# Self attention of a decoder layer: keys, values and scales prepared in the same block as the row loop, tile by tile

## What is computed

```python
def attn(q, k, v):                      # q = layernorm(x)
    step = s // 4
    scale = q[:, ::step].reshape(b, -1) # 4 rows of each batch, 2048 numbers
    qk = jnp.einsum('bsd,btd->bst', q, k)
    softmax_qk = jax.nn.softmax(qk * scale[:, None, :], axis=-1)
    return jnp.einsum('bst,btv->bsv', softmax_qk, v)
x = x + attn(layernorm(x), K, V)
```

## Time and profile before

| | |
|---|---|
| median of 3 runs | 4042.1 us (4041.01 to 4042.7) |
| the profiled execution, its own time | 4039.45 us |
| its span in the profile | 4037.6 us |
| mean granted TensorE clock | 0.976 of full speed |
| TensorE busy over the span | 3803.5 us (94%) |
| VectorE, ScalarE, GpSimd busy | 2418.4, 1424.2, 1483.0 us |
| first block (setup) | 2.1 to about 59.8 us |
| second block (32 tiles) | 59.8 us to about 850 us |
| the rest: context, cross attention, experts | about 850 to 4037.6 us |

### The profile page before, as it was taken

The page is one execution under the profiler, slowest core; times in us unless marked ns, Lnnn a source line. Parts: engine busy times, 40 slices in busy tenths (PEclk is TensorE's granted clock), DMA queues, the critical chain, the costliest instruction groups (busy, mean ns, idle before and its releaser), DMA issues. The chain is left out here.

```text
span 4037.6 us, 63533 instructions
## 1 busy us (share of the span) xinstructions
PE 3803.5 (94%) x19001; PEld 2549.3 (63%) x19161; DVE 2418.4 (60%) x6231; ACT 1424.2 (35%) x1757; POOL 1483.0 (37%) x827
## 2 busy tenths in 40 slices
PE   4999999979997899999999999999999999997997
PEld 3888888868875544454444444444444777776885
DVE  5444444434446677887878888888887434324235
ACT  2221122223222254544545554555555222113332
POOL 1000000000002566677666667766664221310033
PEclk7999999989998999999999999999999999998999
DMA  3001100035546521122222222222111433318488
GB/s 135 31 31 36 34 31 31 31 132 186 177 159 181 146 44 39 35 48 55 55 55 55 55 55 52 55 55 55 44 30 40 159 120 114 124 63 289 164 292 285
DMA packets 224152, 381.61 MB, mean 95 GB/s; under 512 B 17016, under 2 KB 101528, under 8 KB 223900
## 3 DMA queue, kind: packets, MB, share of 16 engines
q1 hardware_dynamic: 196668, 309.73, 26.3%
q0 software_dynamic: 13120, 43.00, 2.9%
q10 hardware_dynamic: 14112, 25.70, 1.7%
HBM read 229.71 MB, written 148.66 MB: 94 GB/s over the span
## 5 line engine op out<-in xcount | busy, mean ns | idle before, releaser
L960 DVE CUSTOM_DVE_ANT_0 xf_unread<-xa_mx_ps,mask_q 128x402 bf16<-128x402 f32 x1984 | 1033.6, 573 | 302.2 <-PE xa_mx_ps L953 164.5
L1547 ACT ACTIVATE probs<-xa_scores 128x1024 f32<-128x1024 f32 (+1 forms) x416 | 417.5, 1024 | 416.4 <-PE xa_scores L1421 371.2
L1547 ACT ACTIVATE xa_probs<-xa_scores 128x1024 f32<-128x1024 f32 (+1 forms) x416 | 417.2, 1024 | 405.6 <-PE xa_scores L1421 360.3
L1382 POOL TENSOR_TENSOR xa_sums<-xa_sums,xa_probs 128x1024 f32<-128x1024 f32 x220 | 519.5, 2382 | 20.0 <-POOL xa_sums L1382 15.0
L1382 POOL TENSOR_TENSOR xa_sums<-xa_sums,probs 128x1024 f32<-128x1024 f32 x220 | 519.4, 2381 | 18.1 <-POOL xa_sums L1382 14.1
L1421 PE MATMUL xa_scores<-mask_t,ident_b 128*128 128x512 bf16 (+1 forms) x1505 | 499.8, 387 | 5.2 <-issue 0.2
L953 PE MATMUL xa_mx_ps<-xa_kp,queries 96*128 96x402 f32 x1024 | 364.6, 418 | 0.8
L953 PE MATMUL xa_mx_ps<-xf_kp,xf_qp 96*128 96x402 f32 x960 | 343.7, 419 | 0.4
L1415 PE MATMUL xa_scores<-xf_qp,xf_kp 97*128 97x512 f32 (+1 forms) x832 | 284.2, 423 | 20.9 <-ACTq L1569 13.4
L953 PEld LDWEIGHTS xa_mx_ps<-xa_kp,queries 96*128 96x128 f32 x1024 | 181.8, 189 | 169.3 <-DVE xf_maxima L960 109.2
L1415 PE MATMUL xa_scores<-queries,xa_kp 97*128 97x512 f32 (+1 forms) x832 | 284.5, 423 | 1.8 <-ACT probs L1547 1.8
(11 more groups left out here) (332 smaller groups left out, 7379.3 us busy)
## 6 DMA issues: line engine op xcount, KB each, us to landing
ex_src<-sorted_in SPq DMA_DIRECT2D x78, 256.0 KB, 2.7
sorted_out<-ex_made ACTq DMA_DIRECT2D x78, 256.0 KB, 2.5
xf_kp<-kT_high SPq DMA_DIRECT2D x16, 800.5 KB
xa_kp<-kT_high SPq DMA_DIRECT2D x16, 800.5 KB
cxl_rows<-in_ctx SPq DMA_DIRECT2D x16, 768.0 KB, 5.7
values<-cxl_v SPq DMA_DIRECT2D x48, 256.0 KB
kT_high<-cxl_kT_high SPq DMA_DIRECT2D x12, 768.0 KB, 4.0
kT_low<-cxl_kT_low SPq DMA_DIRECT2D x12, 768.0 KB, 6.2
```

What stands on the lines that cost most here:

```text
L960: return dve.tensor_tensor_reduce(out=unread[slot % 2][:, :], in0=scores[:, 0:MKEYS], in1=mask_q[:, half * QB + qt, MFIRST[kb]:MFIRST[kb] ...
L1382: pool.tensor_tensor(sums[pr][:, :, :], left[pr][:, :, :], right[pr][:, :, :], ALU.add).then_inc(pool_added, 1)
L1547: act.activation(prob[ring][pr][0:keys, :, :], scores[pr][0:keys, :, :], ACT.Exp, scale=SCALE).then_inc(exped, 1)
```

## The change

One block in place of two. K and V are loaded in 32 tiles of 256 KB into a ring of seven buffers of 2 KB a partition: the four quarters of `prob`, `out`, `x_add` and a new `spare`. K's transposes go through three PSUM banks that the loop uses later (`pT_ps` 0 and 1, `o_ps`) instead of eight. The first tile's scores stand between the transposes of K. The scale rows are loaded batch by batch: those of batch 0 behind the first four tiles of K, the others (1 MB each) behind V. The statistics and the normalization of batches 1 to 3 stand inside tiles 0 to 3 of VectorE, which are written out for this. `exp(0)` waits until all of V is split, since it writes the buffers that V comes through. The low part of V is subtracted tile by tile, the even ones by VectorE, the odd ones by GpSimd.

```diff
-        self_attention_setup(nc, ident, x, k, v, kT, vs, scale)
-        self_attention_loop(nc, ident, x, x1, kT, vs, scale, NB, KB, tiles)
+        raw = [prob[:, j, :] for j in range(NB)] + [out[:, :], x_add[:, :], spare[:, :]]
+        k_ps = [pT_ps[0][:, :, :], pT_ps[1][:, :, :], o_ps[:, :].rearrange("p (c n) -> p c n", n=P)]
...
+                def load_raw(m):
+                    gone = m - RAWS
+                    if 0 <= gone < T1C:
+                        sp.wait_ge(k_turned, gone + 1)
+                    elif gone >= T1C:
+                        sp.wait_ge(v_low_pool if gone % 2 else v_low, (gone - T1C) // 2 + 1)
+                    source = one(k_t, m) if m < T1C else one(v_t, m - T1C)
+                    sp.dma_start(raw[m % RAWS], source).then_inc(raw_in[m % RAWS], 16)
...
                 load_norm(0)
-                load_norm(1)
-                with sp.Fori(0, tiles - 2) as t:
+                for m in range(2 * T1C):
+                    load_raw(m)
+                    if m == KB - 1:
+                        load_scale(0)
+                    if m == 2 * KB:
+                        load_norm(1)
+                load_norm(2)
+                for b in range(1, B):
+                    load_scale(b)
+                wait_v_split(sp)
+                load_add(0)
+                store(0)
+                with sp.Fori(0, tiles - 3) as t:
...
+                step(0)
+                scale_step(0)
+                step(1)
+                for i in range(1, T1C, 2):
+                    pool.wait_ge(v_high, i + 1)
+                    pool.tensor_tensor(vs[1][:, i, :], raw[(T1C + i) % RAWS], words(vs[0][:, i, :]),
+                                       ALU.subtract).then_inc(v_low_pool, 1)
+                for b in range(1, B):
+                    step(b + 1)
+                    scale_step(b)
...
+                def turn_k(i):
+                    wait_raw(pe, i)
+                    if i >= len(k_ps):
+                        pe.wait_ge(k_low, i - len(k_ps) + 1)
...
+                for i in range(KB):
+                    turn_k(i)
                 turn(0)
                 for j in range(NB):
+                    for i in range(KB * (j + 1), KB * (j + 2)) if j + 1 < NB else ():
+                        turn_k(i)
+                    pe.wait_ge(k_low, KB * (j + 1))
                     score(0, j)
                 turn(1)
-                with pe.Fori(0, tiles - 2) as t:
-                    tile(t, 2)
+                tile(0, 2)
+                with pe.Fori(0, tiles - 3) as t:
...
-                high_n(0)
-                high_n(1)
+                for i in range(T1C):
+                    high_k(i)
+                    if i == KB - 1:
+                        high_n(0)
+                for i in range(T1C):
+                    high_v(i)
+                    if i == 6:
+                        high_n(1)
+                wait_v_split(act)
                 exp(0)
...
+                def scale_group(b, j):
+                    if j == 0:
+                        dve.wait_ge(scale_in[b], 16)
+                    dve.bn_stats(scale_stats[:, j, :], scale[:, b, j, :])
+                    if j == NB - 1:
+                        dve.wait_ge(scale_ready, b)
+                        dve.drain()
+                        for g in range(NB):
+                            dve.bn_aggr(scale_mean_var[:, g, :], scale_stats[:, g, :])
+                        dve.drain()
+                        dve.tensor_scalar_add(scale_var[:, :], scale_mean_var[:, :, 1], EPS).then_inc(scale_stat, 1)
...
+                def next_scales(t, j):
+                    if isinstance(t, int) and 0 < t < B:
+                        scale_normal(t, j)
+                    if isinstance(t, int) and t + 1 < B:
+                        scale_group(t + 1, j)
...
                         for j in range(NB - 1):
                             scale_block(t + 1, j)
+                            next_scales(t, j)
                     low_p(t, 0)
                     low_p(t, 1)
...
                         low_n(t + 2)
+                    next_scales(t, NB - 1)
                     low_p(t, 2)
...
                 normalize(0)
+                for i in range(KB):
+                    low_k(i)
                 low_n(0)
+                for j in range(NB):
+                    scale_group(0, j)
+                for i in range(KB, 2 * KB):
+                    low_k(i)
+                for j in range(NB):
+                    scale_normal(0, j)
+                scale_block(0, 0)
+                for i in range(2 * KB, 3 * KB):
+                    low_k(i)
                 normalize(1)
-                for j in range(NB):
-                    scale_block(0, j)
+                scale_block(0, 1)
+                for i in range(3 * KB, 4 * KB):
+                    low_k(i)
+                scale_block(0, 2)
+                for i in (0, 2):
+                    low_v(i)
+                scale_block(0, 3)
                 row_max(0)
+                for i in (4, 6):
+                    low_v(i)
                 low_n(1)
-                with dve.Fori(0, tiles - 2) as t:
+                for i in range(8, T1C, 2):
+                    low_v(i)
+                for t in range(B):
                     tile(t, 2)
+                with dve.Fori(0, tiles - 2 - B) as t:
+                    tile(t + B, 2)
```

More of the change, by code:

```diff
@@ L99, in self_attention @@
     tiles = TOK // P
-    with ExitStack() as keep:
-        sb, _, _ = allocator(keep, nc, "sa")
+    SPREAD = B
+    rows_of_scale = x.rearrange("b (j r) n -> b j r n", j=NB)[:, :, 0, :]
+    k_t, v_t = tokens(k[0]), tokens(v[0])
+    x_t, x1_t = tokens(x.rearrange("b s n -> (b s) n")), tokens(x1)
+    with ExitStack() as ctx:
+        sb, ps, sem = allocator(ctx, nc, "sa")
         kT = [sb(f"kT_{part}", [P, DC, T1], F32R) for part in ("high", "low")]
@@ L231, in self_attention_loop @@
-def self_attention_loop(nc, ident, x, x1, kT, vs, scale, NB, KB, tiles):
-    x_t, x1_t = tokens(x.rearrange("b s n -> (b s) n")), tokens(x1)
-    with ExitStack() as ctx:
-        sb, ps, sem = allocator(ctx, nc, "sal")
         x_norm, x_add = sb("x_norm", [P, D]), sb("x_add", [P, D])
@@ L310, in turn @@
                     last.then_inc(turned, 1)
+                def turn_k(i):
+                    wait_raw(pe, i)
+                    if i >= len(k_ps):
+                        pe.wait_ge(k_low, i - len(k_ps) + 1)
+                    for dc in range(DC):
+                        last = pe.transpose(k_ps[i % len(k_ps)][:, dc, :], raw[i % RAWS][:, dc * P:(dc + 1) * P], ident[:, :])
+                    last.then_inc(k_turned, 1)
                 def score(t, j):
@@ L331, in weigh @@
                         pe.wait_ge(summed, t + 2)
+                    if isinstance(t, int) and t == 0 and j == 0:
+                        wait_v_split(pe)
                     pe.wait_ge(pT_low, NB * t + j + 4)
```

160 lines of the change are left out of this document (51 added, 109 removed).

## The result

The changed kernel takes 4001.06 us (median of 4 runs, 3997.59 to 4003.48) against 4042.4 us of the kernel before (4 runs, 4041.01 to 4046.03). The ratio is 0.9896, 95% interval 0.9879 to 0.9913: 41 us, or 1.0%, faster. The forecast was 4003 us.

What follows compares the result with a forecast made beforehand. TensorE, 94% busy, was taken as the bound, its idle time in the opening as the target: 84.1 - 41 - 4 = 39 us less than 4039.45 gives 4000.4; that execution lies 2.65 under the median, hence 4003 us; range 3998 to 4014.

Steps and rivals of the forecast that it cites:

- S: Start of tile 1's scores on TensorE: 84.08 us before, forecast about 41, bounds 39 and 48.
- The opening: Steps up to tile 1's scores: first K transpose 5.8 us, score(0,0) ending at 20.3, K tiles not held by loads.
- One sign that I had named as wrong: In the opening: transposes of K waiting longer for loads than for banks would show the forecast wrong.
- The low clock before tile 1: Tile 1's three scores on TensorE: 9.9 us instead of 8.2, with the same low-clock stretch as before, some 3.5 us.
- V and exp(0): End of the opening: V all split at about 47 us, exp(0) over at 49.2, needed at 51, covered by 1.7.
- rival 2: Behind tile 1's scores: V's ring ends at 52 instead of 47, exp(0) sets the pace; gain about 35, 4007 us; chance 0.12.
- The first tiles: Tiles 0 to 3: VectorE's added scale steps lose 0.8 + 2 x 1.4, rounded up to 4 us, bounds 1.5 and 7.
- Rival 1: Tile 0's scores: the clock stays low through all of them; S 7 us later, gain 32, 4010 us; chance 0.12.
- Rival 3: K and V loads: small loads do not overlap, 2.6 us for each of 32 tiles; about 8 us slower, 4050; chance 0.03.
- Rival 4: The loop: the opening's 39 us are given back over 31 tiles, 1.3 us each; no change, 4042 us; chance 0.03.
- The stages behind: Everything behind self attention keeps its length; a later stage of another length would show the forecast wrong.

Runs made afterwards that it cites:

- the repeat: The changed kernel itself measured once more, unedited, on another chip: 4003.56 us against 4046.61 for the kernel before there, ratio 0.9891.
- the ring of two: The changed kernel with two buffers instead of seven in the ring of K and V: 4022.07 us, ratio 0.9954 to the kernel before.
- the run that lost 14 us: The changed kernel with all 16 low parts of V on VectorE and one wait fewer on TensorE, ScalarE and SyncE: 4016.3 us, ratio 0.992.
- the reordered kernel: The changed kernel with only VectorE's order changed: low_n(1) before row_max, scale steps of tiles 0 to 3 around low_p 3: 3996.96 us, ratio 0.988.

## Why the prediction was right

**Where the time lay.** The forecast rested on S, the first score of tile 1, and on the loss behind it: 84.1 - 41 - 4 = 39. Measured: 84.08 - 40.85 - 3.7 = 39.5 at the last output, and 40.5 over the profiled executions. In the repeat it is 84.08 - 41.79 - 5.7 = 36.6. The mechanism and its two terms were right; that the first execution agrees to half a microsecond is partly luck.

**The opening.** First transpose 5.59 us (5.8 forecast), statistics of batch 0 over at 15.8 (14.2), score(0,0) from 17.33 (15.7), low parts and banks as the pace from there on, no wait for loads past tile 4. One sign that I had named as wrong did show: in sum over the 16 tiles the transposes waited longer for loads (3.1 us) than for banks (1.9 us). The loads of tile 1 and of batch 0's scales came later than worked out (VectorE waits 1.14 us for tile 1), which is most of the later start. Score(0,0) was over by 21.1 (20.3), since the low pace, which I had priced at 1.9 us, held for its first matmuls only: it took 3.8 us instead of 2.7, so 1.0 us. What VectorE loses beside GpSimd, 1.45 and 1.77 us for a low part, was in the sum as 1.0 on average: 3.22 for the first pair instead of 2.0, but 0.60 each for the second. S came out within 0.2 us, with a start 1.6 us later and a faster middle, so part of that is luck; the repeat has 41.79.

**The low clock before tile 1.** I took 3.5 us of it as before; it was 5.7. With it the three scores took 11.0 us (40.85 to 51.86) instead of 9.9.

**V and exp(0).** V was split at 48.1 (47 forecast), exp(0) over at 50.25 (49.2). It was covered, by 1.6 us. In the repeat it was over at 51.40, and TensorE wanted it at 51.46: rival 2, in which TensorE waits for exp(0), was nearly reached. Even so VectorE's steps behind exp(0) came late, and tile 0 lost 4.1 us there (30.35 against 26.26).

**The first tiles.** 4 us were forecast, 3.7 measured (5.7 in the repeat), and leaving the steps out gave 3.4 back. The split among the tiles was off: tile 0 lost 2.3 (0.8 forecast), tiles 1 and 2 lost 0.5 and 0.7 (1.4 each), tile 3 nothing, as said. In tile 0 the wait ahead of weigh was 1.15 us where 0.8 was forecast, and 1.1 us came from a term that I had at nothing, the longer stretch of low clock. In tiles 1 and 2 the added steps put low_p 0 off by 2.8 us (7.33 us behind the start of normalize, 4.52 in the steady loop), not by 3.2 to 3.7, and no wait for low_p 2 is listed. TensorE's only listed wait in the two tiles is 0.30 us ahead of tile 2's weigh, where 1.1 and 0.3 were priced for each.

**The rivals.** Rival 1: the granted clock was 1.00 from 10 to 30 us and 0.99 up to 40, and three of tile 0's four scores went at the full pace. Rival 3: the ring of two shows that such a cost exists, 27.6 us, below four buffers. The Trainium skill's rule of at least 1 MiB per transfer ("DMA: Bandwidth & Descriptors", section Bandwidth) did not decide here: with up to seven transfers of 256 KB in flight, and one of 1 MB among them, 344 GB/s were moved from 10 to 20 us, where the kernel before moved 391. In V's second half ScalarE does wait for loads, 0.9 to 1.4 us at a time, as the forecast had it; the ring of two is the case in which small transfers do not keep up. Rival 4: the outputs of tiles 3 and 4 are 24.3 us apart and later ones 24.14 again; 0.2 us is lost at that place, and nothing more is given back. Two slips of the sums changed nothing: the range takes 45 as the upper bound of S where the opening had 48, and 256 KB in 2.6 us is 101 GB/s, not 98.

**The stages behind.** That they would keep their length was a step of the forecast, and another length was one of its signs of being wrong. In sum they kept it, within 1.0 us, but cross attention ran 1733.5 us before and 1728.0 after (1390.1 to 3123.6, 1350.7 to 3078.7), and later stages gave 4.4 back. Of the 5.5 us, 4.3 are four waits in the kernel before, of 1.0 to 1.3 us each, at the products with V (line 1429), again with nothing to wait for that the profile shows; the changed kernel has none there. Whether they come from placement, as in the run that lost 14 us, was not tried. A forecast of this kind cannot be surer than these few us.

## What to carry to other kernels

Ask which engine sets the pace of an opening, and count what is moved off it: here the 12 scale rows taken off VectorE's list were worth 15 to 19 us of 41, and the interleaving of scores with K at most 2. The rest, some 20 to 26 us, belongs to the one block in place of two and the new order of loads; the timelines show it, but no run here puts it back by itself. Work put into a steady loop costs the excess over the slack at the first step that another engine waits for, so put it behind that step, into the idle time before the tile's last one. When a kernel's time moves by more than the stage that was edited, look at the lengths of the other stages before explaining it: one instruction fewer ahead of cross attention cost it 14 us.

## What the runs showed of the hardware

- Two tensor_tensor subtractions on SBUF, one on VectorE and one on GpSimd, slow VectorE's from 0.60 us up to 1.77 for 128x512; GpSimd's took 1.27, up to 1.73. They take turns rather than share: VectorE's instruction of 34.31 ends at 36.08, 0.55 us behind the end of GpSimd's (33.80 + 1.73 = 35.53), and 0.55 is about what it needs alone. In the kernel before, the one of 128x2048 that takes 5.04 us alongside GpSimd and 2.29 alone ends 2.2 us behind GpSimd's (35.48 + 4.49 = 39.97). Splitting V's low part between the two bought nothing (exp(0) at 48.16 with both, 47.44 with VectorE alone).
- Cross attention loses 1.3 us at each of six jumps back of its hardware loop in waits on TensorE that nothing in the profile explains, and 2.4 us when TensorE's list ahead of it is one instruction shorter, with a low pace behind most of the longer ones. Adding an instruction instead changed little. What of the placement matters was not tried.
- After a gap of 5.40 us TensorE went at the low pace for 5.7 us; after one of 1.41 us (the reordered kernel) it started at the full one, the first matmul 0.50 us long instead of 0.79. The pace can also fall late: in the kernel before, after 3.35 us, it started with 0.49 us and was down to 0.63 at 85.42.
- In the changed kernel's window of 10 to 20 us the granted clock reads 1.00, and so it does from 17.3 to 19.2 us alone, and yet the matmuls of score(0,0) started 0.43 us apart up to 19.18 us (18.33, 18.75, 19.18). The granted clock of a window and the pace in it are not the same reading. With V's low parts on VectorE alone the same 1.9 us read 0.50.
